# A two-layer transformer on one core: down products of two MLP groups summed in PSUM, rings of three, a second layer whose step is spread anew

## The chip, the cores and the metric

The kernel runs on one core of one Trainium2 chip, in one launch. The metric is the device time of an execution in microseconds (us). The kernel before took 887.87 us, the median of three runs (887.71 to 888.42).

The core's engines run side by side, each its own list of instructions in the order in which the program gives them, and wait for one another by semaphores: TensorE (PE, matmuls into the accumulator memory PSUM), VectorE (DVE), ScalarE (ACT), GpSimd (POOL) and SyncE (SP, which only issues DMAs).

## The reference

2048 tokens of width 512 go through two layers, in float32. Layer 0 is adaptive RMS norm, attention with rotary position encoding over blocks of 64 tokens (8 query heads, one key head of 64), and a gated MLP with 2048 inner columns. Layer 1 is an adaptive layer norm, attention with 16 heads of 32 within the same 64 tokens, its keys and values through a latent of 128, and no MLP. Cut to what matters:

```
# layer 0
h = ada_rms(x, cond, ln1_w, ln1_tw)
q, k, v = rope(h @ Wq.T), rope(h @ Wk.T), h @ Wv.T
x = x + softmax(q k^T / 8) v @ Wo.T
h = ada_rms(x, cond, ln2_w, ln2_tw)
x = x + (silu(h @ Wg.T) * (h @ Wu.T)) @ Wd.T
# layer 1
h = layernorm(x) * (1 + scale) + shift
out = x + masked_attention(h) @ Wo1.T
```

rope(x) is x * cos + rotate_half(x) * sin, where rotate_half of (x1, x2) is (-x2, x1).

## The kernel before

**Precision.** Each float32 operand of a large product is split into a high and a low part (ah and al for the activations, guh and gul for the gate and up weights, wdh and wdl for the down weights). `three` (L642 to L645) makes a product of three matmuls: high by high (L643), low by high (L644), high by low (L645). ACT casts the high part, then DVE (of activations) or POOL (of weights) subtracts it from the source for the low one.

**Tiles.** There are 16 tiles of 128 tokens. The MLP works on blocks of four tiles (512 tokens) and, within a block, on 16 groups of 128 inner columns: 64 groups. A group is a gate product and an up product (12 matmuls each, into the PSUM banks BG and BU) and four down products, one for each tile (3 matmuls each, into the two banks BD in turn). ACT takes silu of the gate (`sg`, L1702), DVE multiplies by up (`af`, L1265), ACT and DVE split (`ah` L1710, `al` L1247), and DVE adds each down product to the residual `xres` (L1252): 256 adds. POOL makes gul (L511) and wdl (L516). ah, al, wdh and wdl have two buffers each.

**Order.** Every engine's order is written out by hand. Attention of layer 0 goes tile by tile in steps s = 1 to 15. From s = 5 on, MLP work is put between the parts of a step: `mlp()` is a generator on each engine that yields after each piece, and `fill(pieces, f)` issues f pieces. A group has four: gate, down of the group before for tiles 0 and 1, up, down for tiles 2 and 3. FILL0 gives three fills of four pieces to each step, f1 after the scores and the query, key and value projection, f2 after the output projection of the step before, f3 at the end. Layer 1 has steps u = -1 to 15, with FILL1's five fills up to u = 9; u = -1 has (4, 4, 0, 4, 0), u = 0 to 8 have (4, 2, 2, 2, 2).

**What stands around the fills.** In a step of layer 0, ACT issues the exponential of the softmax (L1643), then `values` (L1631, which casts the values into `bdv` and waits for DVE's rope products, L1188 to L1190), then f1. exp and silu need different tables, so a table load stands before each. At the end of a step POOL's `rstd2` (L467) makes the root for the MLP norm of a tile, ACT's `norm2` (L1668) applies it. POOL's `rope_sum` (L495) adds the two rope products, DVE does so for the key (L1196). DVE turns the probabilities (L1178, in layer 1 L1371), whose transposition DMAs complete through DRAM. At the start of layer 1 POOL makes the low part of layer 1's output weights (`low_w1_out`, L568).

PE's waits in `mlp()`: a gate product waits for silu of the gate before it (m_sg), since it overwrites the bank; an up product for the multiply before it (m_af); a down product for al and wdl.

## Time and profile before

| | |
|---|---|
| median of 3 runs | 887.87 us |
| profiled execution | 887.57 us |
| its span | 885.7 us |
| PE busy | 852.0 us (96%) |
| DVE busy | 631.7 us |
| ACT, POOL busy | 447.2, 406.6 us |

The span is the time from the first to the last instruction of the trace; 1.87 us of the profiled execution lie outside it. A PE that is busy may still be slow: the granted clock is listed beside it. Matmuls overlap, so the time that one takes from PE is the distance between the starts of two.

### The profile page before, as it was taken

To read this page: it belongs to the slowest core of one execution; us is meant where nothing else is said; L and a number is where in the kernel's file an instruction comes from. 1 tells how busy PE (TensorE), PEld (TensorE's weight loads), DVE (VectorE), ACT (ScalarE), POOL (GpSimd) and SP (SyncE) were. 2 spreads that over 40 slices of the span, in tenths; PEclk is the share of its full clock that TensorE was granted. 3 is DMA by queue.
4 is the path that set the end of the run, shared out by engine and by line. 5 is a ranking of instruction groups with operands and counts; after the bars stand their busy time and mean duration, and the time that the engine had idled before them with its cause. 6 is when DMAs were issued, how large, how long until landed. Compare 5 with 4: busy or idle time off the path is not lost.

```text
span 885.7 us, 15530 instructions
## 1 busy us (share of the span) xinstructions
PE 852.0 (96%) x5864; PEld 707.2 (80%) x5864; DVE 631.7 (71%) x1005; ACT 447.2 (50%) x821; POOL 406.6 (46%) x304
## 2 busy tenths in 40 slices
PE   9798999999999999999989899999999999999997
PEld 6686888788788888787878678788888888888885
DVE  6686577677666677677546877887877867868886
ACT  4665444544444444445445564563553654644662
POOL 2456445545545545537444644544534534431331
PEclk9899999999999999999999899999999999999999
DMA  9811535435425435334423446355354354330001
GB/s 348 330 32 37 172 99 159 124 110 160 122 87 168 122 104 154 116 99 151 156 96 90 169 122 185 115 166 156 121 164 139 114 175 142 117 102 13 25 27 36
DMA packets 114298, 113.54 MB, mean 128 GB/s; under 512 B 57520, under 2 KB 80048, under 8 KB 114224
## 3 DMA queue, kind: packets, MB, share of 16 engines
q1 hardware_dynamic: 113504, 112.45, 39.8%
q8 instruction: 47, 0.77, 0.4%
q10 hardware_dynamic: 720, 0.09, 0.1%
q14 instruction: 27, 0.22, 0.1%
HBM read 88.15 MB, written 24.38 MB: 127 GB/s over the span
## 4 chain that ended last, share of the span: by engine, by line
PE 65%; DVE 11%; ACT 9%; issue 8%; POOL 6%; POOLq 0%; DVEq 0%; ACTq 0%
PE ps L643 20%; PE ps L645 19%; PE ps L644 19%; PE ps L757 2%; POOL gul L511 2%; ACT yf L1763 1%; PE ps L918 1%; ACT L1643 1%; POOL wdl L516 1%; DVE al L1247 1%; DVE ex L1232 1%; PE ps L689 1%; DVE af L1265 1%; ACT ah L1710 1%; ACT guh L1688 1%
## 5 line engine op out<-in xcount | busy, mean ns | idle before, releaser
L511 POOL TENSOR_TENSOR gul<-rgu,guh 128x1024 fp32r<-128x1024 f32 x64 | 154.3, 2411 | 217.5 <-ACT guh L1688 217.5
L1252 DVE TENSOR_TENSOR xres<-ps,xres 128x512 f32<-128x512 f32 x256 | 174.3, 687 | 67.3 <-PE ps L645 67.3
L643 PE MATMUL ps<-h2h,guh 128*128 128x512 f32 x512 | 205.0, 400 | 2.1 <-issue 2.1
L645 PE MATMUL ps<-h2l,guh 128*128 128x512 f32 x512 | 200.6, 392 | 0.0
L644 PE MATMUL ps<-h2h,gul 128*128 128x512 f32 x512 | 200.2, 391 | 0.0
L643 PE MATMUL ps<-wdh,ah 128*128 128x512 f32 x256 | 102.3, 399 | 14.7 <-DVE al L1247 14.7
L643 PEld LDWEIGHTS ps<-h2h,guh 128*128 128x128 f32 x512 | 96.5, 189 | 23.1 <-issue 2.5
L645 PEld LDWEIGHTS ps<-h2l,guh 128*128 128x128 f32 x512 | 96.5, 188 | 21.1
L1710 ACT CAST ah<-af 128x512 fp32r<-128x512 f32 x64 | 39.8, 621 | 143.8 <-DVE af L1265 138.2
L644 PEld LDWEIGHTS ps<-h2h,gul 128*128 128x128 f32 x512 | 96.5, 189 | 19.6
L644 PE MATMUL ps<-wdh,al 128*128 128x512 f32 x256 | 100.7, 393 | 0.0
L645 PE MATMUL ps<-wdl,ah 128*128 128x512 f32 x256 | 100.7, 393 | 0.0
L516 POOL TENSOR_TENSOR wdl<-rwd,wdh 128x512 fp32r<-128x512 f32 x64 | 82.5, 1289 | 13.4 <-ACT wdh L1696 13.3
L1265 DVE TENSOR_TENSOR af<-ps,sg 128x512 f32<-128x512 f32 x64 | 44.2, 690 | 48.5 <-issue 25.2
L643 PEld LDWEIGHTS ps<-wdh,ah 128*128 128x128 f32 x256 | 48.5, 189 | 30.0 <-DVE al L1247 20.2
L1688 ACT CAST guh<-rgu 128x1024 fp32r<-128x1024 f32 x64 | 66.9, 1045 | 0.0
L1702 ACT ACTIVATE sg<-ps 128x512 f32<-128x512 f32 x64 | 38.2, 597 | 55.4 <-PE ps L645 55.2
L467 POOL TENSOR_TENSOR stat<-stat,minus_half 128x1 f32<-128x1 f32 x48 | 38.3, 798 | 42.2 <-DVE stat L1133 40.9
L645 PEld LDWEIGHTS ps<-wdl,ah 128*128 128x128 f32 x256 | 48.6, 190 | 10.3
L644 PEld LDWEIGHTS ps<-wdh,al 128*128 128x128 f32 x256 | 48.7, 190 | 9.3
L1247 DVE TENSOR_TENSOR al<-af,ah 128x512 fp32r<-128x512 f32 x64 | 48.1, 752 | 9.8 <-ACT ah L1710 6.0
L549 POOL TENSOR_TENSOR qkr<-u 128x128 f32<-128x128 f32 x16 | 11.9, 745 | 80.7 <-DVE u L1317 80.7
(180 smaller groups left out, 1655.5 us busy)
## 6 DMA issues: line engine op xcount, KB each, us to landing
rgu<-gu SPq DMA_DIRECT2D x64, 512.0 KB, 3.9
rwd<-WdT SPq DMA_DIRECT2D x64, 256.0 KB, 3.7
turned_q<-tq SPq DMA_DIRECT2D x20, 320.0 KB, 2.3
qkT<-turned_q SPq DMA_DIRECT2D x20, 320.0 KB, 3.7
turned_p<-tp SPq DMA_DIRECT2D x9, 512.0 KB, 2.6
pT<-turned_p SPq DMA_DIRECT2D x9, 512.0 KB, 3.8
xt<-xT SPq DMA_DIRECT2D x16, 256.0 KB, 2.7
out<-xres SPq DMA_DIRECT2D x15, 256.0 KB, 4.1
```

Of the source, the lines that this page charges most:

```text
L467: pool.tensor_tensor(col, col, minus_half[:, :], ALU.pow).then_inc(signal, 1)
L511: pool.tensor_tensor(gul[i][:, :], rgu[i][:, :], guh[i][:, :], ALU.subtract).then_inc(m_gul, 1)
L516: pool.tensor_tensor(wdl[i][:, :], rwd[i][:, :], wdh[i][:, :], ALU.subtract).then_inc(m_wdl, 1)
L643: pe.matmul(dst, lh, rh, start=start, stop=False)
L644: pe.matmul(dst, ll, rh, start=False, stop=False)
L645: return pe.matmul(dst, lh, rl, start=False, stop=stop)
L1247: dve.tensor_tensor(al[n % 2][:, :], af[:, :], ah[n % 2][:, :], ALU.subtract).then_inc(m_al, 1)
L1252: dve.tensor_tensor(at, bank(BD[i % 2]), at, ALU.add).then_inc(m_x, 1)
L1265: dve.tensor_tensor(af[:, :], bank(BU), sg[:, :], ALU.mult).then_inc(m_af, 1)
L1688: act.copy(guh[i][:, :], rgu[i][:, :]).then_inc(m_guh, 1)
L1702: act.activation(sg[:, :], bank(BG), ACT.Silu).then_inc(m_sg, 1)
L1710: act.copy(ah[n % 2][:, :], af[:, :]).then_inc(m_ah, 1)
```

## The change

**Pairs.** Groups are taken two at a time (p = 0 to 31). A down product of a tile is six matmuls that sum both groups of the pair in PSUM, and one add follows it: 128 adds. A pair has eight pieces: gate(2p), up(2p), down of tile 0 of the pair before, gate(2p+1), down of tile 1, up(2p+1), down of tile 2, down of tile 3. The first pair has the four without a down. FILL0 and FILL1 are as they were, and there are 256 pieces, as before. So a fill of four is pieces 1 to 4 or 5 to 8: in the even steps of layer 0 f1 is pieces 1 to 4, in the odd ones 5 to 8 (step 5, where the first pair is, apart); in layer 1 f1 is pieces 5 to 8 where u is even and 1 to 4 where it is odd.

**Rings.** ah, al, wdh, wdl have three buffers (`RING`); room comes from one tile txy for tx and ty (with waits between its two users), from the tile cnd, now tq, and from rope tables of half the width. The loads of gate, up and down weights move into a generator of SP.

**Rope.** With half tables, ACT computes two sines where it did four, DVE's rope multiply is two instructions (128x640) where it was three (128x640 and two of 128x320), DVE's key sum and POOL's `rope_sum` are two instructions each, a subtraction and an addition.

**Side engines.** By piece, ACT: 1 silu(2p), wdh(2p); 3 ah(2p), guh(2p+2); 4 silu(2p+1); 8 ah(2p+1), wdh(2p+1), guh(2p+3). DVE: 2 multiply(2p); 3 al(2p), add; 5 add; 6 multiply(2p+1); 7 add; 8 add, al(2p+1). POOL: 1 wdl(2p); 3 gul(2p+2); 8 wdl(2p+1), gul(2p+3). In layer 1 DVE's statistics of the next tile, the scaling and turning of the probabilities, mean_sq2, ACT's square2 and norm2, and POOL's rstd2 move to other places of the step.

In ACT's row, step 6 of layer 0 (ex is the exponential, bdv the values, sg the silu). Before:

```order
L1615 ACTIVATE sq,stat<-xres 128x512 [waits a_ssq]
L1668 ACTIVATE xn2<-xres,stat 128x512 [waits a_rstd2]
L1643 ACT_TABLE_LOAD
L1643 ACTIVATE ex<-ex 128x512 [waits a_ds]
L1631 ACTIVATE bdv1<-ps,stat 64x64 [waits a_ctx,a_rope]
L1631 ACTIVATE bdv1<-ps,stat 64x64 x3
L1710 CAST ah1<-af 128x512 [waits m_al,m_down,m_af]
L1688 CAST guh1<-rgu1 128x1024 [waits ld_gu1,m_up]
L1702 ACT_TABLE_LOAD [waits m_af]
L1702 ACTIVATE sg<-ps 128x512 [waits m_gate]
L1696 CAST wdh0<-rwd0 128x512 [waits ld_wd0,m_down]
L1710 CAST ah0<-af 128x512 [waits m_al,m_down,m_af]
```

After:

```order
L1685 ACTIVATE sq,stat<-xres 128x512 [waits a_ssq]
L1738 ACTIVATE xn2<-xres,stat 128x512 [waits a_rstd2]
L1713 ACT_TABLE_LOAD
L1713 ACTIVATE ex<-ex 128x512 [waits a_ds]
L1701 ACTIVATE bdv1<-ps,stat 64x64 [waits a_ctx,a_rope]
L1701 ACTIVATE bdv1<-ps,stat 64x64 x3
L1771 ACT_TABLE_LOAD [waits m_af]
L1771 ACTIVATE sg<-ps 128x512 [waits m_gate]
L1766 CAST wdh1<-rwd0 128x512 [waits ld_wd0,m_down]
L1777 CAST ah1<-af 128x512 [waits m_al,m_down,m_af]
L1758 CAST guh0<-rgu0 128x1024 [waits ld_gu0,m_up]
L1771 ACTIVATE sg<-ps 128x512 [waits m_af,m_gate]
```

The table load and sg move directly behind bdv; behind them stand wdh, ah and guh of piece 3 and then the sg of piece 4, all in f1.

In POOL's row, the end of step 5 and step 6 (hl is the low part of layer 0's normed input; stat with a_ms2 is rstd2). Before:

```order
L486 TENSOR_TENSOR hl<-xt1,hh 128x512 [waits a_qkv,a_hh]
L511 TENSOR_TENSOR gul0<-rgu0,guh0 128x1024 [waits m_guh]
L516 TENSOR_TENSOR wdl1<-rwd1,wdh1 128x512 [waits m_wdh]
L467 TENSOR_TENSOR stat<-stat,minus_half 128x1 [waits a_ms2]
L467 TENSOR_TENSOR stat<-stat,minus_half 128x1 [waits a_ms]
L475 TENSOR_TENSOR cs0<-cs0,stat 128x128 [waits a_rstd]
L495 TENSOR_TENSOR qr<-t1,t2 128x512 [waits a_tq,a_rope]
L511 TENSOR_TENSOR gul1<-rgu1,guh1 128x1024 [waits m_guh]
L516 TENSOR_TENSOR wdl0<-rwd0,wdh0 128x512 [waits m_wdh]
```

After:

```order
L516 TENSOR_TENSOR hl<-xt1,hh 128x512 [waits a_qkv,a_hh]
L549 TENSOR_TENSOR wdl0<-rwd1,wdh0 128x512 [waits m_wdh]
L544 TENSOR_TENSOR gul1<-rgu1,guh1 128x1024 [waits m_guh]
L497 TENSOR_TENSOR stat<-stat,minus_half 128x1 [waits a_ms2]
L497 TENSOR_TENSOR stat<-stat,minus_half 128x1 [waits a_ms]
L505 TENSOR_TENSOR cs0<-cs0,stat 128x64 [waits a_rstd]
L527 TENSOR_TENSOR qr<-t1,t2 128x8x32 [waits a_tq,a_rope]
L528 TENSOR_TENSOR qr<-t1,t2 128x8x32
L549 TENSOR_TENSOR wdl1<-rwd0,wdh1 128x512 [waits m_wdh]
L544 TENSOR_TENSOR gul0<-rgu0,guh0 128x1024 [waits m_guh]
```

Before, gul stands between hl and wdl, and then rstd2; now both wdl and gul of piece 8 stand directly before rstd2, and qr is two instructions.

In DVE's row, layer 1's step u = 0 (stat with b_rstd is mean_rstd; ex with b_rec the scaling, tp the turning of the probabilities). Before:

```order
L1265 TENSOR_TENSOR af<-ps,sg 128x512 [waits m_ah,m_al,m_up,m_sg]
L1252 TENSOR_TENSOR xres<-ps,xres 128x512 [waits m_down]
L1247 TENSOR_TENSOR al0<-af,ah0 128x512 [waits m_down,m_ah]
L1252 TENSOR_TENSOR xres<-ps,xres 128x512 [waits m_down]
L1345 TENSOR_REDUCE smx1<-ex1 128x8 [waits b_ex] x2
L1347 RECIPROCAL smx1<-smx1 128x16 [waits b_sum]
L1351 TENSOR_TENSOR ex1<-ex1,smx1 128x1024 [waits b_rec]
L1371 STREAM_TRANSPOSE tp<-ex1 128x1024 [waits st_p0,b_p]
L1300 SCALAR_TENSOR_TENSOR stat<-mv0,stat 128x1 [waits b_rstd]
```

After:

```order
L1321 TENSOR_TENSOR xres<-ps,xres 128x512 [waits m_down]
L1311 TENSOR_TENSOR af<-ps,sg 128x512 [waits m_ah,m_al,m_up,m_sg]
L1415 TENSOR_REDUCE smx1<-ex1 128x8 [waits b_ex] x2
L1417 RECIPROCAL smx1<-smx1 128x16 [waits b_sum]
L1370 SCALAR_TENSOR_TENSOR stat<-mv0,stat 128x1 [waits b_rstd]
L1321 TENSOR_TENSOR xres<-ps,xres 128x512 [waits m_down] x2
L1316 TENSOR_TENSOR al1<-af,ah1 128x512 [waits m_down,m_ah]
L1421 TENSOR_TENSOR ex1<-ex1,smx1 128x1024 [waits b_rec]
L1442 STREAM_TRANSPOSE tp<-ex1 128x1024 [waits st_p0,b_p]
```

The instruction that waits for b_rstd stood behind the turning of the probabilities, and now stands ahead of two adds, of al, and of the scaling and the turning.

The diff, cut to its core (the new generators without the old ones, which stand above):

```diff
+RING = 3
 TURN_P0, TURN_Q0, TURN_X2 = HEAD + 1, HEAD + 2, HEAD
+FIRST_WITH_Y = 12
...
-        tx, ty = sb("tx", [P, D]), sb("ty", [P, D])
+        txy = sb("txy", [P, D])
...
+        def downs_before(n):
+
+            return TPB * ((n - RING) // 2 + 1) if n >= RING else 0
...
+            def mlp():
+                for p in range(NP):
+                    yield
+                    if p:
+                        load_gate_up(2 * p + 3)
+                        load_down(2 * p + 1)
+                    load_down(2 * p + 2)
+                    yield
+                    if p:
+                        yield
+                    yield
+                    load_gate_up(2 * p + 4)
+                    if p:
+                        yield
+                    yield
+                    if p:
+                        yield
+                        yield
...
-                    pool.wait_ge(rope_tab, 4)
-                pool.tensor_tensor(cs0[:, t, :, :], cs0[:, t, :, :], stat[:, 1:2, t:t + 1].broadcast_to([P, 2, HD0]),
+                    pool.wait_ge(rope_tab, 2)
+                pool.tensor_tensor(cs0[:, t, :, :], cs0[:, t, :, :], stat[:, 1:2, t:t + 1].broadcast_to([P, 2, HD0 // 2]),
                                    ALU.mult).then_inc(a_cs, 1)
...
-                u, v = (tile[:, :, :, :].rearrange("p c h d -> p (c h d)") for tile in (t1, t2))
-                pool.tensor_tensor(qr[:, 0:D], u[:, 0:D], v[:, 0:D], ALU.add).then_inc(a_qr, 1)
+                u, v = (tile[:, :, :, :].rearrange("p c h d -> p (c h d)")[:, 0:D]
+                        .rearrange("p (h z a) -> p h z a", z=2, a=HD0 // 2) for tile in (t1, t2))
+                to = qr[:, 0:D].rearrange("p (h z a) -> p h z a", z=2, a=HD0 // 2)
+                pool.tensor_tensor(to[:, :, 0, :], u[:, :, 0, :], v[:, :, 1, :], ALU.subtract)
+                pool.tensor_tensor(to[:, :, 1, :], u[:, :, 1, :], v[:, :, 0, :], ALU.add).then_inc(a_qr, 1)
...
+                for p in range(NP):
+                    low_wd(2 * p)
+                    yield
+                    yield
+                    if p + 1 < NP:
+                        low_gu(2 * p + 2)
+                    if p:
                         yield
                     yield
+                    if p:
+                        yield
+                    yield
+                    if p:
+                        yield
+                    low_wd(2 * p + 1)
+                    if p + 1 < NP:
+                        low_gu(2 * p + 3)
+                    if p:
                         yield
...
             for u in range(-1, NT):
                 f1, f2, f3, f4, f5 = FILL1.get(u, (0,) * 5)
                 ready, soon = PREP1.get(u), PREP1.get(u + 1)
-                fill(pieces, min(f1, 2))
                 if u < TAIL:
                     rstd1(u + 2)
-                fill(pieces, f1 - min(f1, 2))
+                fill(pieces, f1)
                 if in_layer(u + 1):
                     rope_sum1(u + 1)
                 if u >= TAIL and in_layer(u + 3):
                 if u == TAIL:
                     fill(pieces, 2)
                 fill(pieces, f2 + f3)
-                fill(pieces, f4)
+                if soon is not None:
+                    rstd2(soon)
                 if in_layer(u + 2):
                     low_y(u + 2)
+                fill(pieces, f4)
                 if ready is not None:
                     low_h2(ready)
-                if soon is not None:
-                    rstd2(soon)
                 if u == -1:
                     low_w1_out()
                 fill(pieces, f5)
...
+            def down(q, i):
+                pe.wait_ge(m_al, 2 * q + 2)
+                pe.wait_ge(m_wdl, 2 * q + 2)
+                if q == 0 and i == 0:
                     pe.wait_ge(a_x, HEAD)
                     pe.wait_ge(ada_done, 4)
+                wait(pe, m_x, q * TPB + i - 1)
+                f = slice(P * i, P * (i + 1))
+                for n in (2 * q, 2 * q + 1):
+                    r = n % RING
+                    mm = three(bank(BD[i % 2]), ah[r][:, f], al[r][:, f], wdh[r][:, :], wdl[r][:, :],
+                               n % 2 == 0, n % 2 == 1)
+                mm.then_inc(m_down, 1)
...
+                pe.wait_ge(m_gul, n + 1)
+                if w == 0:
+                    wait(pe, m_sg, n)
+                else:
+                    wait(pe, m_af, n)
...
+                for p in range(NP):
+                    gate_or_up(2 * p, 0)
+                    yield
+                    gate_or_up(2 * p, 1)
+                    yield
+                    if p:
+                        down(p - 1, 0)
+                    gate_or_up(2 * p + 1, 0)
+                    yield
+                    if p:
+                        down(p - 1, 1)
+                        yield
+                    gate_or_up(2 * p + 1, 1)
+                    yield
+                    if p:
+                        down(p - 1, 2)
+                        yield
+                        down(p - 1, 3)
+                        yield
+                for i in range(TPB):
+                    down(NP - 1, i)
+                    yield
...
+                wait(dve, st_y, 16 * (t - FIRST_WITH_Y + 1))
...
+                for tile, m in ((t1, 0), (t2, 1)):
+                    ins = dve.tensor_tensor(tile[:, :, :, :].rearrange("p c h (z a) -> p c (h z) a", z=2), halves(q),
+                                            tab(m), ALU.mult)
...
+                to = qr[:, D:D + 2 * HD0].rearrange("p (i z a) -> p i z a", i=2, z=2)
+                dve.tensor_tensor(to[:, :, 0, :], key(t1, 0), key(t2, 1), ALU.subtract)
+                dve.tensor_tensor(to[:, :, 1, :], key(t1, 1), key(t2, 0), ALU.add).then_inc(a_kr, 1)
...
+                for p in range(NP):
+                    yield
+                    multiply(2 * p)
+                    yield
+                    low_act(2 * p)
+                    if p:
+                        add_down(p - 1, 0)
+                    yield
+                    if p:
+                        add_down(p - 1, 1)
+                    multiply(2 * p + 1)
+                    yield
+                    if p:
+                        add_down(p - 1, 2)
+                        yield
+                        add_down(p - 1, 3)
+                    low_act(2 * p + 1)
+                    if p:
+                        yield
+                for i in range(TPB):
+                    add_down(NP - 1, i)
...
                     softmax_sub1(u)
                 if ready is not None:
                     turn_x2(ready)
-                if u < TAIL:
-                    stats1(u + 2)
                 fill(pieces, min(f1, 2))
                 if in_layer(u):
                     softmax_sums1(u)
+                if u < TAIL:
+                    mean_rstd(u + 2)
+                fill(pieces, f1 - min(f1, 2))
                 if 0 <= u <= TAIL:
                     softmax_scale1(u)
                 if 0 <= u < TAIL:
                     turn_probs1(u)
-                if u < TAIL:
-                    mean_rstd(u + 2)
-                fill(pieces, f1 - min(f1, 2))
                 if u == TAIL:
                     fill(pieces, 1)
                 if in_layer(u + 1):
...
+            def silu(n):
+                act.wait_ge(m_gate, n + 1)
+                wait(act, m_af, n)
+                act.activation(sg[:, :], bank(BG), ACT.Silu).then_inc(m_sg, 1)
+            def high_act(n):
+                act.wait_ge(m_af, n + 1)
+                wait(act, m_down, downs_before(n))
+                wait(act, m_al, n - RING + 1)
+                act.copy(ah[n % RING][:, :], af[:, :]).then_inc(m_ah, 1)
+                for p in range(NP):
+                    silu(2 * p)
+                    high_wd(2 * p)
+                    yield
+                    yield
+                    high_act(2 * p)
+                    if p + 1 < NP:
+                        high_gu(2 * p + 2)
+                    if p:
+                    silu(2 * p + 1)
+                    yield
+                    if p:
+                        yield
+                    yield
+                    if p:
+                        yield
+                    high_act(2 * p + 1)
+                    high_wd(2 * p + 1)
+                    if p + 1 < NP:
+                        high_gu(2 * p + 3)
+                    if p:
...
                     queries1(u + 1)
                 if in_layer(u):
                     high_ctx1(u)
-                fill(pieces, f4)
+                if soon is not None:
+                    square2(soon)
                 if u < TAIL:
                     scale_shift_y(u + 2)
                     high_y(u + 2)
+                fill(pieces, f4)
                 if ready is not None:
                     high_h2(ready)
                 if soon is not None:
-                    square2(soon)
+                    norm2(soon)
                 if u == -1:
                     high_w1_out()
                 fill(pieces, f5)
-                if soon is not None:
-                    norm2(soon)
```

## Rows read from the trace of the kernel before

**Rows 1.** the page: busy time of the engines, and its costliest groups.

```profile
PE 852.0 (96%) x5864; PEld 707.2 (80%) x5864; DVE 631.7 (71%) x1005; ACT 447.2 (50%) x821; POOL 406.6 (46%) x304
...
L511 POOL TENSOR_TENSOR gul<-rgu,guh 128x1024 fp32r<-128x1024 f32 x64 | 154.3, 2411 | 217.5 <-ACT guh L1688 217.5
...
L1252 DVE TENSOR_TENSOR xres<-ps,xres 128x512 f32<-128x512 f32 x256 | 174.3, 687 | 67.3 <-PE ps L645 67.3
...
L1710 ACT CAST ah<-af 128x512 fp32r<-128x512 f32 x64 | 39.8, 621 | 143.8 <-DVE af L1265 138.2
...
L1265 DVE TENSOR_TENSOR af<-ps,sg 128x512 f32<-128x512 f32 x64 | 44.2, 690 | 48.5 <-issue 25.2
...
L1688 ACT CAST guh<-rgu 128x1024 fp32r<-128x1024 f32 x64 | 66.9, 1045 | 0.0
```

**Rows 2.** the waits of PE, one line for each pair of waiter and releaser.

```profile
PE ps L643 <- DVE al L1247: 14.7, 13, 3.9
```

**Rows 3.** the timeline of PE: the longest waits, and spacing behind them.

```profile
83.92 0.47 PE L643 MATMUL ps<-h2h,guh 128*128 128x512 f32 x1 [2.08 <-issue]
...
88.26 0.46 PE L643 MATMUL ps<-h2h,guh 128*128 128x512 f32 x1
...
420.49 0.50 PE L643 MATMUL ps<-wdh,ah 128*128 128x512 f32 x1 [1.74 <-DVE al L1247]
...
453.87 0.79 PE L643 MATMUL ps<-wdh,ah 128*128 128x512 f32 x1 [3.18 <-DVE al L1247]
...
455.31 0.63 PE L643 MATMUL ps<-wdh,ah 128*128 128x512 f32 x1
...
455.74 0.63 PE L644 MATMUL ps<-wdh,al 128*128 128x512 f32 x1
...
492.14 0.80 PE L643 MATMUL ps<-wdh,ah 128*128 128x512 f32 x1 [3.93 <-DVE al L1247]
...
498.04 0.34 PE L644 MATMUL ps<-wqh,yl 128*128 128x384 f32 x1
```

**Rows 4.** busy time and granted clock (PEclk) in one stretch of 5 us.

```profile
490.00:495.00 5.00, 2.86 (x7) 2.31 (x8) 4.84 (x8) 3.95 (x5) 4.70 (x4) 0.62 0.67 212
```

**Rows 5.** timelines of PE, POOL and ACT in layer 0's step 12.

```profile
310.86 0.39 PE L645 MATMUL ps<-wdl,ah 128*128 128x512 f32 x1
...
315.43 0.40 PE L643 MATMUL ps<-h2h,guh 128*128 128x512 f32 x1
...
318.19 0.39 PE L643 MATMUL ps<-wdh,ah 128*128 128x512 f32 x1
...
312.52 0.55 POOL L467 TENSOR_TENSOR stat<-stat,minus_half 128x1 f32<-128x1 f32 x1
...
313.84 1.28 ACT L1643 ACT_TABLE_LOAD   x1
...
315.14 0.63 ACT L1643 ACTIVATE ex<-ex 128x512 f32<-128x512 f32 x1
...
320.11 1.28 ACT L1631 ACTIVATE bdv<-ps,stat 64x64 f32<-64x64 f32 x4 [4.34 <-DVE t L1190]
...
324.29 0.60 ACT L1702 ACTIVATE sg<-ps 128x512 f32<-128x512 f32 x1
```

**Rows 6.** the timeline of DVE: one low part of the activations.

```profile
407.93 1.37 DVE L1247 TENSOR_TENSOR al<-af,ah 128x512 fp32r<-128x512 f32 x1 [0.86 <-ACT ah L1710]
```

**Rows 7.** timelines of POOL and DVE at the start of layer 1.

```profile
486.54 4.99 POOL L568 TENSOR_TENSOR wol<-w1st,woh 128x512 fp32r<-128x512 f32 x4
...
495.45 2.04 DVE L1371 STREAM_TRANSPOSE tp<-ex 128x1024 f32<-128x1024 f32 x1
```

**Rows 8.** timelines of PE and POOL, a start-up step and the last groups.

```profile
69.23 1.39 POOL L495 TENSOR_TENSOR qr<-t 128x512 f32<-128x512 f32 x1 [1.85 <-DVE t L1190]
...
70.67 0.65 PE L717 MATMUL ps<-idn,qr 128*128 128x128 f32 x4
...
799.32 0.41 PE L643 MATMUL ps<-wqh,yh 128*128 128x384 f32 x1 [0.99 <-issue]
```

More of the change, by code:

```diff
@@ L124, in build @@
         ah, al = [], []
-        for i in range(2):
+        for i in range(RING):
             ah.append(sb(f"ah{i}", [P, TB], F32R))
             al.append(sb(f"al{i}", [P, TB], F32R))
+        wdh.append(sb("wdh2", [P, D], F32R))
+        wdl.append(sb("wdl2", [P, D], F32R))
         with ExitStack() as l0:
@@ L784, in x2_T @@
                 mm.then_inc(a_x2T, 1)
-            def down(n, i_from, i_to):
-                pe.wait_ge(m_al, n + 1)
-                pe.wait_ge(m_wdl, n + 1)
-                if n == 0 and i_from == 0:
+            def down(q, i):
+                pe.wait_ge(m_al, 2 * q + 2)
+                pe.wait_ge(m_wdl, 2 * q + 2)
+                if q == 0 and i == 0:
                     pe.wait_ge(a_x, HEAD)
                     pe.wait_ge(ada_done, 4)
-                for i in range(i_from, i_to):
-                    wait(pe, m_x, n * TPB + i - 1)
-                    f = slice(P * i, P * (i + 1))
-                    three(bank(BD[i % 2]), ah[n % 2][:, f], al[n % 2][:, f], wdh[n % 2][:, :],
-                          wdl[n % 2][:, :], True, True).then_inc(m_down, 1)
@@ L1920, in _ @@
                     high_y(u + 2)
+                fill(pieces, f4)
                 if ready is not None:
```

206 lines of the change are left out of this document (80 added, 126 removed).

## The prediction

> **What bounds the kernel now.** First the page's busy times: PE is busy for 852.0 us of 885.7, and no other engine comes near [rows 1]. So an edit pays only where PE stands still or runs slowly, and the 128 adds of 0.687 us that DVE loses (87.9 us) are worth nothing by themselves. Second the waits of PE: down products waiting for the low activations `al` lost 14.7 us in 13 waits, the longest 3.9 [rows 2]. That is the waiting that the change is able to remove. Third PE's timeline at the long ones, for what comes behind: after 453.87 two matmuls stand .43 apart (455.31, 455.74), and in the stretch from 490 the mean granted clock is 0.62 [rows 3, 4], so some matmuls run at the 1.2 GHz level. At 2.4 GHz twelve matmuls take 2.76 (315.43 to 318.19), that is .23 each [rows 5].
>
> What a wait costs in clock, by its length [rows 3]: behind the wait of 1.74 the first matmul lasts .50 and nothing slower follows; behind 2.08 (83.92) the slow stretch lasts to 88.26, behind 3.18 about as long, and behind 3.93 from 492.14 to 498.04. Half of a slow stretch is lost. Its first matmuls are sometimes still fast; so I take 1.6 us behind the first, 1.6 behind the second and 2.8 behind the third. A new wait of about 2.6 us thus costs 0 (as 1.74 did) to 1.6 (as 2.08 and 3.18 did) beyond its own length.
>
> **The change part by part: gains.** A down product now comes two pieces or more after the last `al` that it needs, so the 13 waits go: 14.7 us [rows 2]. The slow stretches behind the two longest go with them: 1.6 + 2.8 = 4.4. At 799.32 PE waits .99 for the last multiply before it can begin a projection [rows 8]; now only downs stand there: 1.0. Sum 20.1 us. PE's own matmuls stay the same in number and size. What is late next is `sg`.
>
> **The new wait, even steps of layer 0.** In the even steps f1 is pieces 1 to 4, and piece 4 is gate(2p+1), which waits for silu(2p). On ACT that silu stands behind the exponential and behind `bdv`, which waits for DVE's rope products. Before, the next gate came only in f2, behind a second down, an up and the output projection. Step 12 as it was, with the new pieces laid on it [rows 5]:
> - PE begins f1 at 315.43. Gate and up are 2.76 each, one down of six matmuls 1.36 (half of 12): it wants gate(2p+1) at 315.43 + 6.88 = 322.3.
> - ACT's bdv begins at 320.11, having waited 4.34 for rope, and lasts 1.28; then a table load, 1.28, and sg, .60: 323.3 with handovers. That is a wait of 1.0 even if nothing else moves.
> - The exponential itself comes later. Before, rstd2 ran at 312.52. Now POOL has wdl and gul of piece 8 ahead of it. The last matmul of up(2p+1) begins 12 matmuls before the last down's, at 310.86 - 2.73 = 308.13, and ends at 308.5; af .69, ah .62, wdh (the size of ah) .62, guh 1.05 and gul 2.41 follow [rows 1], 5.4 us, and about .25 of handovers: rstd2 at 314.16, so 1.64 later. norm2, the exponential's table (313.84, 1.28), the exponential and so rope and bdv all move with it, since they form one chain: bdv waited 4.34 for it.
> - Together 2.65 us. Steps 6, 8, 12 and 14 have this form: 10.6. By the rule of the clock above 0 to 1.6 each behind it; since 2.65 lies between 2.08 and 3.18, both of which were followed by a slow stretch, I take three quarters of 6.4: 4.9. Bounds of both together: 4 x 1.0 = 4.0 (rstd2 not later, no clock) to 17.0.
>
> The odd steps have gate(2p+1) in the step before, and step 10 applies no MLP norm (no rstd2 and norm2), so its exponential isn't held by them and its silu is ready.
>
> By the Trainium skill ("ScalarE: Activation LUTs", section "What ACT_TABLE_LOAD costs") a switch of tables is about 1.28 us of load and 1.38 of drain, 2.66 in all. That rule speaks against this change, since the wait then grows by 1.38 each. The trace doesn't agree: the load at 313.84 lasts 1.28 and the exponential begins at 315.14, 1.30 after it began [rows 5]. By the page the four waits would be 5.5 us more; by the row they are as above.
>
> **Layer 1's step 0.** `low_w1_out` keeps POOL for 4.99 from 486.54 to 491.53 [rows 7], and rstd1 comes behind it, .55 long as rstd2 [rows 5]: 492.2 with a handover. DVE's mean_rstd, which waits for it, now stands ahead of two adds (2 x .69), al (.69), the scaling (of 1024 columns, twice the .69 less one start: 1.3) and the turning (2.04) [rows 1, 7]; behind those come rope (1280 columns at .69 for 512: 1.7), the values (1.28 as bdv), a table and a silu (1.28 + .60) [rows 5]: 502.5. PE's side, counted from rows 3: it was idle for 3.93 before 492.14, so its work ended at 488.2, and gate, down and up had taken 6.9, so f1 began at 481.3. Now f1 is an up and three downs, 6.8; the projection is some 24 matmuls of 384 columns at .17 (three quarters of .23), 4.1; gate, up and one down are 6.9; key transposes about .5: 499.6. A wait of 2.9, of which I count 2.8, as a handover is in both; with three quarters of a slow stretch 1.1 more: 3.9. Bounds: 0 (if the adds were late anyway and POOL is earlier) and 6.
>
> **Low parts beside POOL.** al took 1.37 beside a POOL instruction [rows 6], where its usual time is near the .69 of an equal DVE instruction [rows 1]. In the new order al(2p+1) is issued in the last piece, where POOL starts the 2.41 us gul: in step 10 and in u = 3, 5, 7 the next use is close. Bounds: 0 and 4 x 2.41 = 9.6 (held until gul ends); I take the .68 of the row four times: 2.7. By the Trainium skill ("GPSIMD Engine Reference", section "Key points") GpSimd's SBUF interfaces are shared with VectorE, and instructions with two SBUF inputs contend; the row agrees with that, but it shows the instruction twice as long, not held to the end of POOL's. Held to the end, it would give the 9.6.
>
> **Rope in two.** In the four start-up steps without MLP work POOL's qr ends at 70.62 and PE's transposes of it begin at 70.67 [rows 8]: nothing hides it. Two of half the size cost at least one more start; no row shows POOL with half the columns, but a 128x1 instruction of POOL lasts .55 [rows 5], so one more start is between 0 and .55, and I take .25: 1.0 in four steps. Later the second key instruction on DVE can be delayed by POOL in the odd steps: 0 to 2, taken .7. Step -1 with its moved norm: .3.
>
> **Edits at nothing.** Half tables (two sines less, at the start, where DMAs are awaited), the shared tile txy (its two users write it in different steps or at the two ends of one), the tile tq for cnd, and SP's order are hidden by PE's own work. If a load of weights came late, PE would wait for gul; the rings of rgu and rwd are as before, and they are issued earlier or as early. stats1, square2 and mean_sq2 move within steps of layer 1 in which PE is full.
>
> **The sum.** Losses 10.6 + 4.9 + 3.9 + 2.7 + 1.0 + .7 + .3 = 24.1; gains 20.1; net +4.0. The profiled execution took 887.57, so 891.6, and the median of the runs shown is .3 higher: 892.
>
> **The rivals.**
> - A, the silu waits aren't there: some slack that I don't see (rstd2 not in the way, the exponential earlier) lets sg be in time. Then 887.6 - 20.1 + 4.7 (the small terms 2.7, 1.0, .7 and .3) = 872, and 876 with the wait in step 0. For it speaks only that each wait has a 6.9 us run of PE work ahead of it; against it, that even without rstd2's move sg is 1.0 late. Faster: this is the case on the other side, and it decides if the silu waits are below .8 us each.
> - B, the waits are there at their size, but the clock stays at 2.4 GHz, as behind 1.74 [rows 3]: 892 - 4.9 - 1.1 = 886, with 883 to 888 for the small terms.
> - C, my forecast, 889 to 896 as its own range (all five slow stretches: +1.9; al held by gul in part: +2).
> - D, al is held until gul ends: + 6.9, 899; or a table switch with its drain, about as much. What speaks for it is only the doubled al; against it, its 1.37.
> - E, the change doesn't take away the waits for al, since in layer 1 the ring is exhausted: a down must then wait for wdl, and 14.7 stays: 907. Three buffers are filled at most two groups ahead, and the wait for m_down is for a pair ended two pieces or more earlier; I give it almost nothing.
>
> **How the numbers follow.** A 22%, B 23%, C 48%, D 5%, E 2%. What a measurement of this kernel can tell from no change is about 0.2%, 1.8 us: 886.1 to 889.6. Faster: A, and over half of B, 36%. Same: the rest of B and an edge of C, 12%. Slower: 52%. The range takes in A's upper part and D: 870 to 899.
>
> **What would show it.** Right: PE waits for ACT's `sg` before a gate matmul in steps 6, 8, 12, 14, 2.65 us each, and in step 0 of layer 1; a granted clock below 1 behind them; no wait for `al` of the old size; rstd2 5.6 us after the last up matmul's end in even steps, behind gul; adds 128. Wrong: no line of PE waiting for `sg`, or waits under 1 us, which makes A; clock at 1.00 behind waits of 2.6, which makes B.

## The result and the profile after

The changed kernel took 910.41 us (median of 4 runs, 909.42 to 913.29), the kernel before 887.79 (4 runs, 886.77 to 888.42): a ratio of 1.026, 95% interval 1.024 to 1.029. I had forecast 892 with a range of 870 to 899, so it lies outside the range. The direction and the four places were right, the size was five times too small: 22.6 us, not 4. The profiled execution took 909.91 us, its span is 908.1.

The page of the changed kernel, the lines that answer to those of before [rows 1]:

```profile
PE 855.8 (94%) x5864; PEld 709.5 (78%) x5864; DVE 572.6 (63%) x877; ACT 445.0 (49%) x819; POOL 403.2 (44%) x320
...
L684 PE MATMUL ps<-h2h,guh 128*128 128x512 f32 x512 | 206.2, 403 | 27.9 <-ACT sg L1771 25.6
...
L1321 DVE TENSOR_TENSOR xres<-ps,xres 128x512 f32<-128x512 f32 x128 | 86.8, 682 | 28.4 <-PE ps L686 28.4
```

PE's busy time grew by 3.8 us though its matmuls are the same; the mean granted clock of the two profiled executions fell from 0.988 to 0.983. The rest of the 22.4 us by which the span grew, 18.6, is idle PE. The adds halved, from 174.3 us to 86.8, and brought nothing. Gate matmuls now have 27.9 us of waiting ahead of them, 25.6 of it for `sg`.

The waits of PE (total, times, longest), where before `al` stood with 14.7 us [rows 2]:

```profile
PE ps L684 <- ACT sg L1771: 25.6, 11, 4.6
...
PE ps L684 <- DVE xres L1321: 5.8, 5, 1.7
```

The waits for `al` are gone. In their place come 11 waits for silu and 5 for the residual's add, `xres`. The four longest are 4.58 or 4.59 us, at 128.17, 201.69, 343.25 and 416.77: layer 0's steps 6, 8, 12, 14, as forecast. Step 12 on PE, ACT and POOL (start, duration, in brackets the idle time before it and its releaser); the answers to [rows 5] of before:

```profile
327.10 0.39 PE L686 MATMUL ps<-wdl,ah 128*128 128x512 f32 x1
...
331.67 0.40 PE L684 MATMUL ps<-h2h,guh 128*128 128x512 f32 x1
...
338.28 0.39 PE L686 MATMUL ps<-wdl,ah 128*128 128x512 f32 x1
...
343.25 0.77 PE L684 MATMUL ps<-h2h,guh 128*128 128x512 f32 x1 [4.58 <-ACT sg L1771]
...
344.24 0.63 PE L686 MATMUL ps<-h2l,guh 128*128 128x512 f32 x1
...
344.67 0.63 PE L684 MATMUL ps<-h2h,guh 128*128 128x512 f32 x1
...
327.57 0.62 ACT L1777 CAST ah<-af 128x512 fp32r<-128x512 f32 x1 [3.12 <-issue]
...
332.98 0.72 ACT L1738 ACTIVATE xn<-xres,stat 128x512 f32<-128x512 f32 x1 [2.70 <-POOL stat L497]
...
339.92 1.27 ACT L1701 ACTIVATE bdv<-ps,stat 64x64 f32<-64x64 f32 x4 [4.27 <-DVE t L1250]
...
342.51 0.60 ACT L1771 ACTIVATE sg<-ps 128x512 f32<-128x512 f32 x1
...
328.79 1.30 POOL L549 TENSOR_TENSOR wdl<-rwd,wdh 128x512 fp32r<-128x512 f32 x1 [2.84 <-ACT wdh L1766]
...
330.04 2.40 POOL L544 TENSOR_TENSOR gul<-rgu,guh 128x1024 fp32r<-128x1024 f32 x1
...
332.40 0.55 POOL L497 TENSOR_TENSOR stat<-stat,minus_half 128x1 f32<-128x1 f32 x1
```

f1 begins at 331.67. Its last matmul ahead of gate(2p+1) starts at 338.28, and gate(2p+1) at 343.25, since sg ends at 343.11. The two rows after it are .43 apart: the lower clock. Read the chain backwards: sg, its table load and bdv end to end from 339.92; rope, the exponential, norm2 at 332.98; rstd2 at 332.40, behind gul and wdl; and those behind ah at 327.57. I had worked out rstd2 at 1.27 **before** f1's start; it is .73 behind it. The reason is in the first row: the last matmul of the down of tile 3 starts at 327.10, and ah(2p+1) begins at 327.57, as it ends.

The odd steps, on PE and DVE, here step 7:

```profile
157.38 0.40 PE L684 MATMUL ps<-wdh,ah 128*128 128x512 f32 x1
...
161.06 1.51 DVE L1250 TENSOR_TENSOR t<-ps,cs 128x640 f32<-128x640 f32 x2
...
162.75 0.75 DVE L1259 TENSOR_TENSOR qr<-t 128x64 f32<-128x64 f32 x1
...
163.42 0.68 DVE L1321 TENSOR_TENSOR xres<-ps,xres 128x512 f32<-128x512 f32 x1
...
164.24 0.47 PE L684 MATMUL ps<-wdh,ah 128*128 128x512 f32 x1 [1.22 <-DVE xres L1321]
```

The add of tile 1's down stands behind rope and the key, ends at 164.10, and the down of tile 3 into the same PSUM bank starts at 164.24, 1.22 late. The same step before the change:

```profile
149.87 0.40 PE L643 MATMUL ps<-h2h,guh 128*128 128x512 f32 x1
...
156.49 0.39 PE L645 MATMUL ps<-h2l,guh 128*128 128x512 f32 x1
...
155.38 0.68 DVE L1252 TENSOR_TENSOR xres<-ps,xres 128x512 f32<-128x512 f32 x1
```

There f1 begins at 149.87, the add that frees the bank ends at 156.06, 6.2 later, and the down that needs it stands behind the matmul of 156.49, about 6.9 behind f1's start. Now the add ends 6.7 behind f1's start (157.38), but the down stands only 5.5 behind it: a down of 1.36 has taken the place of a gate of 2.76. Four of the five waits for xres are this (1.22, 1.21, .48 and 1.19, in steps 7, 9, 11 and 13); the fifth, 1.71, is in step 15.

Where the time went, by the two profiles (slow stretches: what matmuls took above .2275 us, .176 and .147 by width, summed):

| | before | after |
|---|---|---|
| waits for al, slow stretches behind them | 14.7, 3.6 | 0, 0 |
| sg in steps 6, 8, 12, 14; slow stretches | 0 | 18.3, 6.3 |
| sg in steps 10 and 14's end, start of layer 1, its step 0 | 0 | 1.2, 1.0, 2.0, 2.3 |
| xres (PSUM bank) | 0 | 5.8 |
| transposed queries by DMA in layer 1 | 0 | 1.0 |
| ahead of the last downs or projection; slow stretch | 1.0, 0 | 1.8, 1.3 |
| slow stretch behind the first gate | 1.7 | 0 |

With the row of the last downs counted by what it grew (.8 and 1.3), the new entries sum to 40.0 and the ones gone to 20.0: 20.0 of 22.4 us. The other 2.4 I can't place. The 1.7 behind the first gate is luck: the wait there is as long as before (2.19, before 2.08), and the slow stretch behind it comes and goes among the kernels below.

### The profile page after: what moved, and what is told of

It reads as the page before. It is cut to its first block, busy times and chain, and to the rows that moved or that the text cites. A ratio compares the mean times of both kernels' runs of the same rounds, so it can differ in the third digit from the quotient of the medians.

```text
span 908.1 us, 15477 instructions
## 1 busy us (share of the span) xinstructions
PE 855.8 (94%) x5864; PEld 709.5 (78%) x5864; DVE 572.6 (63%) x877; ACT 445.0 (49%) x819; POOL 403.2 (44%) x320
## 4 chain that ended last, share of the span: by engine, by line
PE 65%; DVE 10%; ACT 9%; issue 8%; POOL 5%; DMA 1%; POOLq 0%; ACTq 0%; DVEq 0%; SPq 0%
PE ps L684 20%; PE ps L686 19%; PE ps L685 19%; POOL gul L544 2%; DVE t L1250 2%; PE ps L976 1%; ACT L1713 1%; PE ps L798 1%; ACT guh L1758 1%; DVE ex L1294 1%; PE ps L730 1%; PE ps L953 1%; DVE smx L1289 1%; ACT L1771 1%; ACT ex L1713 1%
## 5 line engine op out<-in xcount | busy, mean ns | idle before, releaser
L684 PE MATMUL ps<-h2h,guh 128*128 128x512 f32 x512 | 206.2, 403 | 27.9 <-ACT sg L1771 25.6
L544 POOL TENSOR_TENSOR gul<-rgu,guh 128x1024 fp32r<-128x1024 f32 x64 | 160.0, 2500 | 33.4 <-ACT guh L1758 33.4
L1321 DVE TENSOR_TENSOR xres<-ps,xres 128x512 f32<-128x512 f32 x128 | 86.8, 682 | 28.4 <-PE ps L686 28.4
L1316 DVE TENSOR_TENSOR al<-af,ah 128x512 fp32r<-128x512 f32 x64 | 52.9, 826 | 12.9 <-ACT ah L1777 12.8
L497 POOL TENSOR_TENSOR stat<-stat,minus_half 128x1 f32<-128x1 f32 x48 | 29.4, 613 | 43.5 <-DVE stat L1191 39.8
```

Source lines behind the costliest of these rows:

```text
L497: pool.tensor_tensor(col, col, minus_half[:, :], ALU.pow).then_inc(signal, 1)
L544: pool.tensor_tensor(gul[i][:, :], rgu[i][:, :], guh[i][:, :], ALU.subtract).then_inc(m_gul, 1)
L684: pe.matmul(dst, lh, rh, start=start, stop=False)
L1316: dve.tensor_tensor(al[n % RING][:, :], af[:, :], ah[n % RING][:, :], ALU.subtract).then_inc(m_al, 1)
L1321: dve.tensor_tensor(at, bank(BD[i % 2]), at, ALU.add).then_inc(m_x, 1)
```

## The experiments

They ran in three groups, each on a chip of its own with the kernel before beside it: the first four (886.26 us before), the next four (886.78) and the last four (886.56). That is 1.5, 1.0 and 1.2 us less than in the comparison above, to be taken off where a time is set against the 910.41. Each time is the median of 4 to 10 runs.

**Silu ahead of the values.** ACT, layer 0:

```diff
+                ahead = 1 if s > HEAD + 1 and s % 2 == 0 else 0
+                fill(pieces, ahead)
                 if in_layer(s + 1):
                     values(s + 1)
-                fill(pieces, f1)
+                fill(pieces, f1 - ahead)
```

> The changed kernel, but in the even steps of layer 0 from 6 on ACT issues piece 1 (silu(2p), wdh(2p)) ahead of values, in the idle time between the exponential and bdv. Theory 1 (PE's waits for sg come from silu(2p) standing behind bdv, whatever made bdv late): the four waits of 4.58 us and the 1.15 of step 10 go, and with them the slow stretches behind them (1.2, 1.9, 1.2, 1.9): 25.7 us less than 910.4, 884.7. Rival (the chain only moves on: the multiply or ah(2p) and guh wait in its place): waits of 2 us or more stay in those steps, 892 or more.

Measured: 883.34 us, ratio to before 0.999 (0.997 to 1.000).

```profile
PE ps L684 <- ACT sg L1771: 6.1, 6, 2.3
...
PE ps L684 <- DVE xres L1321: 5.8, 5, 1.7
```

All five sg waits of the even steps and their slow stretches are gone: 27.1 us less, 25.6 when the 1.5 between the comparisons is taken off, for one piece moved past another. Theory 1 stands; the rival falls.

**rstd2 ahead of the fill.** POOL, layer 0:

```diff
+                if s > HEAD and soon is not None:
+                    rstd2(soon)
                 fill(pieces, f3)
-                if s > HEAD and soon is not None:
-                    rstd2(soon)
```

> The changed kernel, but in layer 0 POOL issues rstd2 of the next step ahead of fill f3, so ahead of wdl and gul of piece 8. Theory 1 (the chain rstd2, norm2, exponential, rope, bdv, sg sets the wait): norm2 can begin when ACT has made guh and sq, at 330.3 in place of 333.0 in step 12, so each wait falls from 4.58 to 1.9: 10.7 us less, and 0 to 6.2 of slow clock: 893.5 to 899.7. Rival (POOL's place doesn't matter since ACT or the exponential is late by itself): 908 or more.

Measured: 885.0 us, 0.999 (0.998 to 1.001): 25.4 us less than the changed kernel, 23.9 without the difference between the comparisons, and lower than both theories.

```profile
PE ps L684 <- ACT sg L1771: 11.8, 10, 2.3
...
PE ps L684 <- DVE xres L1321: 1.7, 1, 1.7
...
327.84 0.47 PE L684 MATMUL ps<-h2h,guh 128*128 128x512 f32 x1 [1.78 <-ACT sg L1771]
```

The sg wait of step 12 is 1.78 (worked out: 1.9), but I had missed three things. The rope chain is earlier in the odd steps too, so their add is in time: xres fell from 5.8 to 1.7. The wait of 1.96 for sg at the start of layer 1, which stood behind norm2 and rstd2 too, is gone. And the profile shows no slow stretch behind waits of 1.78. By the profile that is 11.8 for the four waits (the one in step 14 fell to 1.17), 2.0, 4.1 and 6.3.

**The ring.** The down products of tiles 2 and 3 take the second group of the pair twice (their result isn't the sum), so a slot is free two downs earlier:

```diff
-            return TPB * ((n - RING) // 2 + 1) if n >= RING else 0
+            if n < RING:
+                return 0
+            return TPB * ((n - RING) // 2) + 2 if n % 2 else TPB * ((n - RING) // 2 + 1)
...
-                    r = n % RING
+                    r = n % RING if i < 2 else (2 * q + 1) % RING
```

> The changed kernel, but the down products of tiles 2 and 3 read the second group of the pair twice and the first not at all (its share of the sum is left out, the matmuls stay six), so the ring slots of group 2p-2 are free after the down of tile 1, and ah(2p+1), al and wdh(2p+1) no longer wait for the down of tile 3. Theory 1 (the 1.93 us that each wait is longer than I worked out, 4.58 against 2.65, is this wait for the ring, which I had left out): ah in step 11's end begins 1.9 us earlier, rstd2 as well, each of the four waits is 2.6, 7.8 us less: 902.6, and lower by up to 3 where the clock recovers sooner. Rival (the excess is POOL and DVE in each other's way, or DVE's longer rope part): the waits stay above 4, 909 to 911.

Measured: 898.7 us, 1.016 (1.013 to 1.018), 11.7 less than the changed kernel, 10.2 without the difference between the comparisons.

```profile
323.55 2.40 POOL L546 TENSOR_TENSOR gul<-rgu,guh 128x1024 fp32r<-128x1024 f32 x1
...
325.90 1.00 POOL L499 TENSOR_TENSOR stat<-stat,minus_half 128x1 f32<-128x1 f32 x1
...
323.62 2.87 DVE L1318 TENSOR_TENSOR al<-af,ah 128x512 fp32r<-128x512 f32 x1
...
327.16 0.40 PE L686 MATMUL ps<-h2h,guh 128*128 128x512 f32 x1
...
337.21 0.76 PE L686 MATMUL ps<-h2h,guh 128*128 128x512 f32 x1 [3.05 <-ACT sg L1773]
```

rstd2 begins at 325.90, 1.26 before f1's start at 327.16: the place that I had worked out without the ring (1.27). With the ring it stands .73 behind f1's start, so the ring moves it by 2.0, which is the whole excess of 1.93. The wait is 3.05 all the same, not 2.65, since a new delay takes .4 of it back: al starts at 323.62 beside gul (323.55 to 325.95) and lasts 2.87, against a mean of .75 in the kernel before, and rstd2, which begins beside it, lasts 1.00 in place of .55. norm2 begins as rstd2 ends. The rival (contention alone) falls; that contention adds to it is shown.

The time fell by more than the four waits (4 x 1.53 = 6.1). In that profile the waits for sg at the start of layer 1 and in its step 0 are gone as well (2.0 and 2.3), the last downs wait .5 in place of 1.8, and the waits for the queries by DMA grew from 1.0 to 4.0.

**The add ahead of rope**, DVE, odd steps of layer 0:

```diff
+                ahead = 1 if s > HEAD + 1 and s % 2 else 0
+                f1 -= ahead
+                fill(pieces, ahead)
                 if in_layer(s + 1):
                     rope_mul(s + 1)
```

> The changed kernel, but in the odd steps of layer 0 from 7 on DVE issues piece 5 (the add of tile 1's down) ahead of the rope multiply, not behind it. Theory 1 (PE's waits for xres, 5.8 us in 5, are for that add, which frees the PSUM bank that the down of tile 3 needs, and which stands behind DVE's rope work): they go, 904.6. Rival (the add is late because of DVE's second key instruction of .74 us, which POOL holds up): the add ahead of rope removes that too, but rope, bdv and qr come .7 later and PE waits for them: 909 or more.

Measured: 906.67 us, 1.025 (1.022 to 1.028).

```profile
PE ps L684 <- ACT sg L1774: 25.6, 11, 4.6
...
PE ps L684 <- DVE xres L1321: 1.6, 1, 1.6
```

The four waits of the odd steps went, 4.1 us; step 15's (1.6) stayed, since what stands ahead of its add is the softmax's scaling and turning. So theory 1 holds for the waits, but for that one. The time fell by 3.7, or 2.2 without the difference between the comparisons, and not by 5.8: the slow stretches behind the four sg waits took 8.0 in this profile (6.3 in the other), and 1.7 stood behind the first gate.

**Both moves in layer 0**, silu and rstd2.

> Both single moves at once in layer 0: ACT's silu(2p) ahead of values in the even steps, POOL's rstd2 ahead of fill f3. Theory 1 (one late chain, rstd2 to rope, costs PE twice: through sg in the even steps and through the add for the PSUM bank in the odd ones): rstd2 first takes away the bank waits of the odd steps (4.1 us that silu first had left) and the wait of 1.96 at the start of layer 1; silu first takes away the 7.7 us of sg waits that rstd2 first had left. Either way the sum is 877.3. Rival (the two take away the same time, the rest is a clock that differs from run to run): 883 to 885, as each alone.

Measured: 876.8 us, 0.989 (0.987 to 0.991).

```profile
PE ps L684 <- ACT sg L1771: 4.1, 5, 2.3
...
PE ps L684 <- DVE xres L1321: 1.7, 1, 1.7
```

The first version that is clearly faster than the kernel before, at the time worked out from the two single runs (877.3).

**Silu ahead of the values in layer 1 as well**, the same edit before `values1`.

> As the one with both moves, and in the even steps of layer 1 ACT issues piece 1 (silu(2p), wdh(2p)) ahead of values1. Theory 1 (the wait of 2.32 us for sg in step 0 of layer 1 is silu(2p) behind the values, which wait for rope behind mean_rstd and the output weights' low part): it goes, with 0 to 1.6 of slow clock: 2.3 to 3.9 below the kernel with both moves, 873.4 to 875. Rival (POOL's 5 us of output weights delay al and gul as well, so that another wait comes in its place): no more than 0.5 below.

Measured: 877.8 us, 0.990 (0.987 to 0.993).

```profile
PE ps L684 <- ACT sg L1771: 1.8, 4, 1.0
...
PE ps L953 <- DMA qkT<-turned_q: 1.8, 1, 1.8
...
PE ps L976 <- DMA pT<-turned_p: 1.7, 1, 1.7
```

The rival is right in the time: the 2.3 us for sg went, and 1.75 and 1.72 of waiting for the transposition DMAs of queries and probabilities came. They are not the waits for al and gul that it named. That DVE turns the probabilities late is the likely reason, as it does so behind POOL's output weights; no run shows it by itself. That a wait is named is no proof that its removal pays.

**Silu ahead of the cast of layer 1's query weights** too, at the end of step 14.

> As the one with layer 1's silu ahead, and at the end of step 14 ACT issues piece 1 ahead of the cast of layer 1's query weights (1.91 us). Theory: the wait of .96 for sg there goes; the cast, and POOL's 5.5 us behind it, come .6 to 1.1 later, so the bank wait of 1.71 in step 15 grows by at most as much: -1.0 to +0.2 against the kernel without this move. Rival (POOL's long low part then meets DVE's scaling of the probabilities in full): slower by 1 or more.

Measured: 881.59 us, 0.995 (0.993 to 0.997), slower than without it by about 4.

```profile
PE ps L684 <- DVE xres L1321: 3.3, 1, 3.3
...
418.58 0.16 DVE L1370 SCALAR_TENSOR_TENSOR stat<-mv,stat 128x1 f32<-128x1 f32 x1 [1.63 <-POOL stat L497]
```

The sg wait of .96 went, and the bank wait in step 15 grew from 1.71 to 3.3, with a slow stretch of 2.5 behind it. The rival has the time right (slower by 1 or more), but not the way: the scaling lasts .83, so it doesn't meet POOL in full. The add starts at 418.65, behind mean_rstd, which had waited 1.63 for POOL's rstd1; and that stands behind the low parts of the query weights, wdl and gul.

**The rope part alone** in the kernel before.

> The kernel before with one part of the change alone: half rope tables, DVE's rope multiply and POOL's sum in two halves each, the key in two instructions. I had put it at 1.7 us (1.0 in the start-up, .7 later). Theory 1 (nearly nothing in the start-up, since the changed kernel's first MLP matmul came at 84.01 in place of 83.92; the key's .75 us delays af and al by about .5 in the steps where al is waited for): +0.1 to +3. Rival (the rope part is what made the chain late in the changed kernel, through contention): + 5 or more.

Measured: 886.5 us, 1.000 (0.999 to 1.001).

```profile
PE ps L646 <- DVE al L1253: 16.1, 13, 3.9
```

The waits for al grew by 1.4 us in that profile, the time didn't measurably. The rope part alone is not the cause of the slowdown.

**mean_rstd back behind the turning in layer 1's step 0:**

```diff
-                if u < TAIL:
+                if u < TAIL and u != 0:
                     mean_rstd(u + 2)
...
                     turn_probs1(u)
+                if u == 0:
+                    mean_rstd(u + 2)
+                    fill(pieces, f1 - min(f1, 2))
```

> The kernel with both moves in layer 0 (876.8), and in layer 1's step 0 DVE's mean_rstd and the last two pieces of f1 stand behind the scaling and the turning of the probabilities, as mean_rstd did before the change. Theory 1 (the wait of 2.32 for sg there, and the waits for the transposition DMAs that took its place when silu alone was moved, both come from DVE being held for POOL's 5 us of output weights): the turning ends about 3.3 us earlier, sg is in time and no DMA is waited for: 2.3 us less, and up to 1.8 of slow clock: 872.7 to 874.5. Rival (al and the two adds now come so late that PE waits for them): 876 or more.

Measured: 875.24 us, 0.989 (0.985 to 0.992): no clear difference to 876.8. sg still waits 1.44, and 2.41 for the queries by DMA. POOL and DVE there:

```profile
486.82 2.39 POOL L544 TENSOR_TENSOR gul<-rgu,guh 128x1024 fp32r<-128x1024 f32 x1
...
487.18 2.05 DVE L1370 SCALAR_TENSOR_TENSOR stat<-mv,stat 128x1 f32<-128x1 f32 x1
```

mean_rstd, a single column, lasts 2.05 and ends with POOL's gul (489.21). The scaling of the probabilities, now beside POOL's output weights, lasts 2.35 in place of 1.21. So DVE lost again most of what the move gained: of the 3.3 that I expected sg came .9 earlier. Inconclusive as to the time; whether taking POOL's output weights elsewhere pays was not tried.

**The last group outside the ring**: ah, al, wdh, wdl of group 63 go to `guh[0]` and `gul[0]`, which are free by then, and DVE makes the last al ahead of the last add of the pair before. ACT's part for ah, of an edit on four engines:

```diff
+                if n == NN - 1:
+                    act.wait_ge(m_up, NN - 1)
+                    act.copy(guh[0][:, 0:TB], af[:, :]).then_inc(m_ah, 1)
+                    return
                 wait(act, m_down, downs_before(n))
...
```

> The kernel with both moves in layer 0, and the last group (63) puts ah, al, wdh and wdl not into the ring but into the free tiles of gate and up weights, so that nothing of it waits for the last down of the pair before. Theory 1 (PE's wait of 1.81 us ahead of the last four downs is the ring again: ah began when the down of tile 3 ended, then wdh, wdl): it goes, and the slow stretch of 1.7 behind it: 1.8 to 3.5 less, 873.3 to 875. Rival (POOL's low weights are late by POOL's own work): the wait stays above 1.

Measured: 872.25 us, 0.984 (0.982 to 0.987), below the 873.3 to 875 of theory 1. The kernel with both moves, and below it this one:

```profile
497.05 0.72 PE L684 MATMUL ps<-h2h,guh 128*128 128x512 f32 x1 [2.32 <-ACT sg L1771]
...
780.97 0.62 ACT L1777 CAST ah<-af 128x512 fp32r<-128x512 f32 x1 [3.16 <-PE ps L686]
...
782.18 1.26 POOL L549 TENSOR_TENSOR wdl<-rwd,wdh 128x512 fp32r<-128x512 f32 x1 [3.01 <-ACT wdh L1766]
...
783.54 0.52 PE L684 MATMUL ps<-wdh,ah 128*128 128x512 f32 x1 [1.81 <-issue]
```

```profile
496.27 0.47 PE L688 MATMUL ps<-h2h,guh 128*128 128x512 f32 x1 [2.32 <-ACT sg L1791]
...
780.71 0.50 PE L688 MATMUL ps<-wdh,ah 128*128 128x512 f32 x1 [0.36 <-DVE guh L1325]
```

The wait fell from 1.81 to .36 and no slow stretch of 1.7 follows: 3.1 us, within the 1.8 to 3.5 of theory 1. It is the ring again, in a kernel that computes all of its sums. The time fell by 4.6. Most of the rest is luck: behind the wait of 2.32 in layer 1's step 0, which is the same in both, the kernel with both moves has a slow stretch of 1.6 in its profile and this one has none.

**The add in step 15** ahead of the softmax's sums, and **all of the moves**.

> The kernel with both moves in layer 0, and in step 15 DVE issues piece 5, the add of tile 1's down, ahead of the softmax's sums. Theory 1 (the bank wait of 1.71 there is the add behind the scaling, which POOL's 5.5 us of query weights stretch to 1.94, and the turning): it goes, 875.1. Rival (DVE then is late with the turning or with yn, and PE waits there): 876.5 or more.

> All of the moves together: silu and rstd2 in layer 0, mean_rstd in layer 1's step 0, the last group outside the ring, the add in step 15. By the theory the waits are independent and add up: 2.3 + 1.8 + 1.7 off 876.8, and 0 to 3.5 of slow clock: 867.5 to 871. Rival (one stands in for the other): 873 or more.

Measured: 875.27 us, 0.987 (0.984 to 0.991), with the bank wait gone as expected, though its runs (871.98 to 876.31) overlap those of the kernel without this move (876.03 to 877.41); and 870.77 us, 0.983 (0.980 to 0.986).

```profile
PE ps L688 <- ACT sg L1798: 3.3, 5, 1.5
```

All of the moves have the lowest median: 1.7% faster than the kernel before and, by the two ratios, 4.2% faster than the changed one, all by the place of instructions and, for the last group, of its buffers. The runs (869.55 to 872.46) overlap those with the last group outside the ring (871.65 to 872.68), so what the last two moves add is not shown. The waits aren't independent either: in layer 1's step 0 sg still waits 1.46, with 1.06 for the queries by DMA behind it.

## Why the prediction was wrong in its size

- **The gains** were right: al's 14.7 us went, and 3.6 of slow clock (I took 4.4). The 1.0 at the end went too, but the ring put 1.8 and a slow stretch of 1.3 in its place.
- **The step that failed** is "af .69, ah .62, wdh (the size of ah) .62, guh 1.05 and gul 2.41 follow". It lets ah begin when af is there. But group 2p+1's slot in a ring of three is that of group 2p-2, the first of the pair whose downs are being issued, so ah and wdh wait for the down of tile 3, two downs after up(2p+1). By the ring experiment that puts rstd2 2.0 us later and makes each wait 1.5 longer (4.58 against 3.05; the other .4 is what rstd2 beside DVE costs there). I had looked at this wait only in rival E ("a pair ended two pieces or more earlier"), which is true of group 2p and false of 2p+1. Four times 4.58 in place of 2.65 is 7.7 us.
- **Step 10** I had put at nothing ("its silu is ready"), because no rstd2 holds its exponential. It waits 1.15, as it does with rstd2 first (1.16), and not with silu first. My own sum had 1.0 for sg "even if nothing else moves", and that applies to step 10 as well.
- **The bank wait** of xres: I had .7, it is 5.8. I counted the key instruction's delay, and not that the down which reuses the bank now stands 1.4 us nearer to f1's start, while the add still stands behind rope. It hangs on the same late chain, since rstd2 first took away four of five.
- **Left out of the sum**: at the start of layer 1 the first silu stands behind norm2 of tile 12, which waits for POOL's rstd2 (2.0), and at the end of step 14 a silu stands behind the cast of the query weights (1.0). Neither norm2 nor the cast moved; what comes behind them did. PE has no work behind the wait there: "PE is full" held for the kernel before, not for the new order.
- **The clock**: I had 4.9 behind the four waits, the profile shows 6.3. Rightly sized. Behind step 0's wait I had 1.1, and that profile shows none.
- **Terms that were too high**: rope in the start-up, nothing measurable for 1.0 (the first gate at 84.01, before 83.92; and the rope part alone at 1.000). Low parts beside POOL, no wait for al at all for 2.7.
- **Layer 1's step 0**: 2.3 for 2.8, by the chain that I had laid out. ACT and PE there:

```profile
528.12 1.08 ACT L1866 COPY bdv<-ps 64x128 f32<-64x128 f32 x4 [6.75 <-DVE u L1387]
...
530.50 0.60 ACT L1771 ACTIVATE sg<-ps 128x512 f32<-128x512 f32 x1
...
531.25 0.47 PE L684 MATMUL ps<-h2h,guh 128*128 128x512 f32 x1 [2.32 <-ACT sg L1771]
```

  Between the two ACT rows stands only a table load; gate(2p+1) starts as sg ends.
- **Rivals**: A fell with the waits themselves, B with the slow stretches behind all four, E with the waits for al. Of D the holding is real, but no down waited for al. I had also misread [rows 6]: al, which begins at 407.93 and lasts 1.37, stood beside this instruction of POOL,

```profile
407.45 1.30 POOL L560 TENSOR_TENSOR wql<-w1st,wqh 128x512 fp32r<-128x512 f32 x1 [0.51 <-ACT wqh L1722]
```

  and ended .55 behind it (409.30 against 408.75). The row showed what I denied, an al held to the end of POOL's instruction.

Added up, the misses fit: too low by 7.7, 1.4, 5.1, 4.1 (step 10 and the two left out), 3.1 (the last downs), 1.0 (queries by DMA) and .8 (gains), too high by 2.7, 1.0, 1.6 (step 0 with its clock), .3 (step -1), and 1.7 of luck behind the first gate. That is 15.9, and with the 2.4 that I can't place the 18.3 between 891.6 and 909.9.

## What to carry to other kernels

When buffers turn in a ring and are freed by groups, write down for each member of the group which instruction frees its slot and where that stands in the piece; a ring of three under pairs is a ring of two for every second group. When one engine's late chain delays several others, moving its head (one instruction on POOL, 25.4 us) pays at several places at once. Moving a victim (silu, 27.1 us) can pay as much, but only where nothing else that is bound to the same chain waits next; in layer 1 it paid nothing. Judge a reordering by what waits in the new order, not by how full PE was in the old one.

## What the runs showed of the hardware

A DVE instruction with two inputs in SBUF that begins while a subtraction of POOL runs is held until that one's end, even when it is a single column: 2.05 us for mean_rstd, from 487.18 to 489.23 beside a gul that ends at 489.21; and al ends .54 behind gul's end in the ring experiment. In the changed kernel's trace al begins so 17 times, beside wdl as a rule, and ends .55 behind POOL's end each time. An add with one input in PSUM isn't held: the one at 130.51 lasts .68 and ends 1.65 before the gul beside it. It runs the other way too: POOL's rstd2 took 1.00 in place of .55 where it began beside al. The Trainium skill says that such instructions contend ("GPSIMD Engine Reference", section "Key points"); the trace agrees, and here shows for how long.

The clock behind a wait isn't told by the wait's length. The 1.8 us ahead of the last downs were followed by 1.7 us of slow stretch in the profile of the kernel with both moves and by none in that with the add in step 15; the 2.32 us in layer 1's step 0 by 1.6 and by none; 1.75 us for the DMA in layer 1 by 1.7; the 1.78 us in layer 0 of the kernel with rstd2 first by none. So a sum from one profile carries an uncertainty of some 1.7 us for each such wait.
